# A chain of twelve layers on one core: first fetches and filter preparation inside the first stage, two middle stages joined in one block

## The reference

```
x = _layernorm(x + _L0_attn_ref(x, ...))     # stage 0: 16 heads, table of relative biases
x = _layernorm(x + _L0_xattn_ref(x, ...))    # stage 1: top-32 attention, then s4d
x = _layernorm(x + _L0_ffn_ref(x, ...))      # stage 2: slots
x = _layernorm(x + _L1_attn_ref(x, ...))     # stage 3: linear attention, across the 32 sequences
x = _layernorm(x + _L1_xattn_ref(x, ...))    # stage 4: 8 heads of 64, cross attention
...
def s4d(x, log_dt, A_re, A_im, C_re, C_im, D_skip):
    dtA = dt[:, None] * A
    dC = C * (jnp.exp(dtA) - 1.0) / A
    powers = jnp.exp(dtA[:, :, None] * jnp.arange(L))
    K = 2.0 * jnp.einsum('dn,dnl->dl', dC, powers).real
```

## Time and profile before

| | |
|---|---|
| median of 3 runs | 3241.17 us (3241.14 to 3243.67) |
| the profiled execution | 3240.98 us, its span 3239.2 us |
| PE busy | 2693.2 us (83%) |
| DVE busy | 1952.7 us (60%) |
| ACT busy | 1381.1 us (43%) |
| POOL busy | 1318.9 us (41%) |

### The profile page before, as it was taken

One profiled execution on the slowest core, in us unless ns is written; L12 is line 12 of the kernel. 1 busy time (PEld: TensorE's weight loads), 2 busy tenths in 40 slices (PEclk: granted clock), 3 DMA queues, 4 the chain that ended last, 5 costly groups with the idle time before them and its releaser, 6 DMA issues. The chain is left out here.

```text
span 3239.2 us, 78330 instructions
## 1 busy us (share of the span) xinstructions
PE 2693.2 (83%) x31738; PEld 1918.6 (59%) x31745; DVE 1952.7 (60%) x5135; ACT 1381.1 (43%) x3100; POOL 1318.9 (41%) x1379
## 2 busy tenths in 40 slices
PE   6992566666676999899899986998979999979986
PEld 3551333444534776565799975566357777755665
DVE  5997999355763444566544444564856666635665
ACT  4551556354444554344322213553134444425544
POOL 3451556263311112554233333453843333334546
PEclk9996677687787999899899997998999999989988
DMA  3000000400000000100000000001000000000000
GB/s 105 3 2 1 1 1 1 106 11 1 7 1 34 2 2 2 42 2 3 8 1 1 1 1 17 2 2 44 1 6 2 2 2 2 2 8 2 3 1 27
DMA packets 25350, 37.31 MB, mean 12 GB/s; under 512 B 696, under 2 KB 22336, under 8 KB 24128
## 3 DMA queue, kind: packets, MB, share of 16 engines
q1 hardware_dynamic: 24992, 32.30, 3.2%
HBM read 30.07 MB, written 2.23 MB: 10 GB/s over the span
## 5 line engine op out<-in xcount | busy, mean ns | idle before, releaser
L1205 POOL TENSOR_TENSOR L_attn__qk<-L_attn__turned 128x512 f32<-128x512 f32 x128 | 161.7, 1274 | 300.6 <-DVE L_attn__turned L1316 300.6
L787 DVE TENSOR_REDUCE L_xattn__nm<-psum 128x8 bf16<-128x1024 f32 x128 | 156.4, 1224 | 149.5 <-PE psum L982 143.3
L4346 PE MATMUL psum<-L_ffn__e_hT,weights 128*128 128x256 f32 x1024 | 244.8, 383 | 0.0
L1316 DVE TENSOR_TENSOR L_attn__turned<-psum,weights 128x1024 f32<-128x1024 f32 x128 | 153.4, 1218 | 91.8 <-PE psum L1423 88.8
L4346 PEld LDWEIGHTS psum<-L_ffn__e_hT,weights 128*128 128x128 f32 x1024 | 186.8, 192 | 20.6
L4200 DVE TENSOR_TENSOR L_ffn__e_a<-L_ffn__e_sg,psum 128x512 f32<-128x512 f32 x128 | 88.0, 687 | 176.6 <-ACT L_ffn__e_sg L4192 176.5
L4192 ACT ACTIVATE L_ffn__e_sg<-psum 128x512 f32<-128x512 f32 x128 | 76.5, 598 | 258.7 <-PE psum L4346 258.7
L727 ACT ACTIVATE L_xattn__pT<-psum 128x1024 f32<-128x1024 f32 x128 | 124.0, 1021 | 58.8 <-PE psum L1010 58.8
L4359 PEld LDWEIGHTS psum<-weights,L_ffn__e_a 128*128 128x128 f32 x1024 | 134.4, 191 | 7.3 <-DVE L_ffn__e_a L4200 0.7
L1423 PE MATMUL psum<-L_attn__xT,weights 128*128 128x256 f32 x512 | 136.2, 399 | 2.0 <-DVE L_attn__turned L1316 1.3
L4359 PE MATMUL psum<-weights,L_ffn__e_a 128*128 128x128 f32 x1024 | 135.1, 275 | 0.5 <-DVE L_ffn__e_a L4200 0.5
(11 more groups left out here) (680 smaller groups left out, 7512.9 us busy)
## 6 DMA issues: line engine op xcount, KB each, us to landing
L_xattn__conv_toeplitz<-s4d_kernel SPq DMA_DIRECT2D x5, 1024.0 KB, 10.5
weights<-pack SPq DMA_DIRECT2D x1, 3328.0 KB, 10.6
weights<-pack SPq DMA_DIRECT2D x1, 3140.0 KB, 9.9
weights<-s4d_kernel SPq DMA_DIRECT2D x3, 1024.0 KB, 9.1
weights<-pack SPq DMA_DIRECT2D x1, 2370.0 KB, 9.0
out_dram<-X SPq DMA_DIRECT2D x8, 256.0 KB, 2.3
weights<-pack SPq DMA_DIRECT2D x1, 1732.5 KB, 14.5
ctxT<-ctxT_in SPq DMA_DIRECT2D x1, 1536.0 KB, 18.7
```

What stands on the lines that cost most here:

```text
L787: nc.vector.tensor_reduce(nm[:, n % 2, :].rearrange("p (g c) -> p g c", g=4)[:, 2 * u:2 * u + 2, 0:4], scores[u].rearrange("p g (i q) -> p ...
L1205: nc.gpsimd.tensor_tensor(qk[:, p % 2, u], turned[:, g % 2, :, 0:2 * P], turned[:, g % 2, :, 2 * P:4 * P], ALU.add).then_inc(qk_sb, 1)
L1316: nc.vector.tensor_tensor(turned[:, g % 2], proj[u % 2].unsqueeze(1).to_broadcast([P, 2, 4 * P]), k.w(name + "rope").rearrange("p (t q) -> ...
L4346: last = nc.tensor.matmul(bank[g % 2][:, 256 * c:256 * c + 256], k.w(name + w)[:, o:o + P], hT, start=True, stop=True)
```

## The change

It has three parts, and all twelve stages compute the same as before.

1. `load_stage` is gone. Its work stands in a class `Opening`, whose pieces stage 0's engines run. The packed tensor is cut finer ("const", "s4d", "bias", "later"), SP issues the first pair of X and the small pieces ahead of the bias tables, and the wait for each transfer stands at its first use.
2. The preparation block of stage 1 is gone. DVE works out the angles ahead of stage 0's loop (`dve_angles`), ACT takes sine and cosine once in the loop (`act_waves`), and all else (the powers, the coarse factors, the small tables) goes to POOL, cut into parts 1 to 14: part p stands in POOL's queue of stage 0 behind `with_bias(p + 1)`.
3. Stages 3 and 4 share one block. The statistics, roots and outputs of stage 3's units 1 to 7 (`TurnedTail`) move into stage 4's queues: unit 1 ahead of its loop, units 2 to 7 in it at fixed places. The residuals are written into YT, which holds all units.

The diff, cut to its core:

```diff
+    @contextmanager
+    def one_block(self):
+
+        with ExitStack() as memory, self.nc.Block() as block:
+            self.shared = (memory, block)
+            yield
+        self.shared = None
...
-def load_stage(k):
-
-    nc = k.nc
-    with nc.Block() as block:
-
-        @block.sync
-        def _(sp):
-            k.load_weights(sp, "const")
-            k.load_weights(sp, STAGES[0])
-            xs = k.x.rearrange("b t d -> t b d")
-            sp.dma_start(k.X[:, 0:8, :], xs[:, 0:8, :]).then_inc(k.x_loaded, 16)
-            sp.dma_start(k.X[:, 8:NB, :], xs[:, 8:NB, :]).then_inc(k.x_rest, 16)
-            sp.dma_start(k.ctxT[:], k.ctxT_dram).then_inc(k.ctx_loaded, 16)
...
+    def sync(self, sp):
+        k = self.k
+        xs = k.x.rearrange("b t d -> t b d")
+        k.load_weights(sp, "const")
+        sp.dma_start(k.X[:, 0:2, :], xs[:, 0:2, :]).then_inc(k.x_first, 16)
+        k.load_weights(sp, "s4d")
+        k.load_weights(sp, 0)
+        k.load_weights(sp, "bias")
+        sp.dma_start(k.X[:, 2:8, :], xs[:, 2:8, :]).then_inc(k.x_loaded, 16)
+        sp.dma_start(k.X[:, 8:NB, :], xs[:, 8:NB, :]).then_inc(k.x_rest, 16)
+        sp.dma_start(self.mask_keys[:], k.masks[1][0].rearrange("(u j) g -> u (j g)", j=4)).then_inc(self.masks_in, 16)
+        sp.dma_start(self.mask_text[:], k.masks[0]).then_inc(self.masks_in, 16)
+        k.load_weights(sp, "later")
+        sp.dma_start(k.ctxT[:], k.ctxT_dram).then_inc(k.ctx_loaded, 16)
...
+    def act_waves(self, act):
+        scalar = self.k.nc.scalar
+        act.wait_ge(self.angles, 1)
+        scalar.activation(self.mag[:], self.a_re[:], ACT.Exp)
+        scalar.activation(self.sn[:], self.ang[:], ACT.Sin)
+        scalar.activation(self.cs[:], self.cang[:], ACT.Sin).then_inc(self.waves, 1)
...
+    def pool_part(self, pool, p):
+        k, nc, w, NN, FINE = self.k, self.k.nc, self.w, self.NN, self.FINE
+        tt, ts, copy = nc.gpsimd.tensor_tensor, nc.gpsimd.tensor_scalar, nc.gpsimd.tensor_copy
+        pw, ws = self.pw, self.ws
+
...
+        def multiplied(a, b, m):
+            q = [t[:, 0:m * NN].rearrange("p (m n) -> p m n", n=NN) for t in self.prod]
+            tt(q[0], a[0], b[0], ALU.mult)
+            tt(q[1], a[1], b[1], ALU.mult)
+            tt(q[2], a[0], b[1], ALU.mult)
+            link(tt(q[3], a[1], b[0], ALU.mult))
+
+        def combined(out, m):
+            q = [t[:, 0:m * NN].rearrange("p (m n) -> p m n", n=NN) for t in self.prod]
+            tt(out[0], q[0], q[1], ALU.subtract)
+            link(tt(out[1], q[2], q[3], ALU.add))
...
+        if p == 2:
+            pool.wait_ge(self.waves, 1)
+            pool.wait_ge(self.inverse, 1)
+            tt(pw[0][:, 1, :], self.mag[:], self.cs[:], ALU.mult)
+            link(tt(pw[1][:, 1, :], self.mag[:], self.sn[:], ALU.mult))
+            ts(self.z1[:], pw[0][:, 1, :], 1.0, None, ALU.subtract)
+            link(ts(self.conj[:], w("A_im"), -1.0, None, ALU.mult))
+            times([one(a[:]) for a in self.g], (one(self.z1[:]), pw[1][:, 1:2, :]),
+                  (one(w("A_re")), one(self.conj[:])), 1)
+            for c in range(2):
+                last = tt(self.gi[c][:], self.g[c][:], self.inv[:], ALU.mult)
+            link(last)
+            for c in range(2):
+                last = ts(self.h[c][:], self.gi[c][:], 2.0, None, ALU.mult)
+            link(last)
+            times([a[:, 0:1, :] for a in ws], [one(a[:]) for a in self.h], (one(w("C_re")), one(w("C_im"))), 1)
+        if p == 3:
+            times([a[:, 2:3, :] for a in pw], *doubled(1), 1)
+            times([a[:, 3:5, :] for a in pw], *doubled(2), 2)
+        if p == 4:
+            times([a[:, 5:9, :] for a in pw], *doubled(4), 4)
+        if p == 5:
+            multiplied(*doubled(8), 8)
+        if p == 6:
+            combined([a[:, 9:17, :] for a in pw], 8)
+            times([a[:] for a in self.q2], q, q, 1)
+        if p == 7:
+            times([a[:] for a in self.q4], [a[:] for a in self.q2], [a[:] for a in self.q2], 1)
+            coarser(1, q)
+        if p == 8:
+            coarser(2, [a[:] for a in self.q2])
+        if p == 9:
+            coarser(4, [a[:] for a in self.q4])
...
+                            if opening:
+                                opening.pool_part(pool, p)
...
+                if opening:
+                    pe.wait_ge(k.loaded["const"], 16)
+                else:
+                    pe.wait_ge(k.loaded[stage], 16)
+                    if not rope:
+                        value_bias()
                 turn(0)
+                if opening:
+                    pe.wait_ge(k.loaded[stage], 16)
                 if cross:
                     pe.wait_ge(k.ctx_loaded, 16)
                 if rope:
...
+                if bias:
+                    act.wait_ge(k.loaded["bias"], 16)
+                    nc.scalar.activation(bias16[:], k.w(name + "bias_qk"), ACT.Copy).then_inc(bias16_sb, 1)
...
+                sp.wait_ge(*before.weights_read)
...
+                    pool.wait_ge(before.x_out, p // 2 + 1)
...
+                before.root(pool, 1)
                 for p in range(NB // 2):
+                    if p + 2 in LATE:
+                        before.root(pool, p + 2)
...
+                before.block_out(act, 1)
...
-                        for s in range(2):
-                            evict_v(p + 1, s)
+                        evict_v(p + 1, 0)
+                        for u, at in LATE.items():
+                            if n == at + 3:
+                                before.block_out(act, u)
+                        evict_v(p + 1, 1)
...
+                before.shifted(dve, 1)
                 maxima(0)
                 for n in range(NB):
                     if n + 1 < NB:
                         maxima(n + 1)
+                    for u, at in LATE.items():
+                        if n in (at, at + 1):
+                            before.statistics(dve, range(4 * u + 2 * (n - at), 4 * u + 2 * (n - at) + 2))
+                        if n == at + 2:
+                            before.shifted(dve, u)
                     inverted(n)
...
+                    pe.wait_ge(before.x_out, p // 2 + 1)
+                    if p == 0:
+                        pe.wait_ge(before.res_sb, 3)
...
+    def statistics(self, dve, sequences):
+        vector = self.k.nc.vector
+        for i in sequences:
+            dve.wait_ge(self.res_sb, i // 4 + 1)
+            vector.bn_stats(self.st[:, i, :], self.r[:, i, :]).then_inc(self.halves, 1)
+        for i in sequences:
+            dve.wait_ge(self.halves, i + 1)
+            vector.bn_aggr(self.mv[:, i, :], self.st[:, i, :]).then_inc(self.moments, 1)
+
+    def root(self, pool, u):
+        k, gpsimd = self.k, self.k.nc.gpsimd
+        pool.wait_ge(self.moments, 4 * u + 4)
+        gpsimd.tensor_tensor(self.rstd[:, u, 0, :], self.mv[:, 4 * u:4 * u + 4, 1],
+                             k.eps[:, 0:1].to_broadcast([P, 4]), ALU.add).then_inc(self.var_eps, 1)
+        pool.wait_ge(self.var_eps, u + 1)
+        gpsimd.tensor_tensor(self.rstd[:, u, 1, :], self.rstd[:, u, 0, :], k.neg_half[:, 0:1].to_broadcast([P, 4]),
+                             ALU.pow).then_inc(self.rstd_sb, 1)
+
+    def shifted(self, dve, u):
+        dve.wait_ge(self.rstd_sb, u + 1)
+        dve.wait_ge(self.moments, 4 * u + 4)
+        self.k.nc.vector.scalar_tensor_tensor(out=self.shift[:, u, :], in0=self.mv[:, 4 * u:4 * u + 4, 0], scalar=-1.0,
+                                              in1=self.rstd[:, u, 1, :], op0=ALU.mult,
+                                              op1=ALU.mult).then_inc(self.shift_sb, 1)
+
+    def block_out(self, act, u):
+        act.wait_ge(self.shift_sb, u + 1)
+        for j in range(4):
+            last = self.k.nc.scalar.activation(self.k.X[:, 4 * u + j, :], self.r[:, 4 * u + j, :], ACT.Identity,
+                                               bias=self.shift[:, u, j:j + 1], scale=self.rstd[:, u, 1, j:j + 1])
+        last.then_inc(self.x_out, 1)
...
-                sp.wait_ge(y_ps, BLOCKS)
+                sp.wait_ge(y_ps, BLOCKS // 2)
...
-                    nc.vector.tensor_tensor(r[:, u % 2], k.bank[u][:].rearrange("p (j d) -> p j d", j=4),
-                                            k.X[:, 4 * u:4 * u + 4, :], ALU.add).then_inc(res_sb, 1)
...
+                    units = slice(4 * u, 4 * u + 4)
+                    nc.vector.tensor_tensor(YT[:, units, :], k.bank[u][:].rearrange("p (j d) -> p j d", j=4),
+                                            k.X[:, units, :], ALU.add).then_inc(res_sb, 1)
+
+                residual(0)
+                tail.statistics(dve, range(0, 4))
+                residual(1)
+                residual(2)
+                tail.shifted(dve, 0)
+                residual(3)
+                residual(4)
+                tail.statistics(dve, range(4, 8))
+                residual(5)
+                residual(6)
+                residual(7)
...
-
-                        m = 1
```

(24 more changed lines are left out.)

486 lines of the change are left out of this document (249 added, 237 removed).

## The result

The changed kernel takes 3186.09 us (median of 4 runs, 3182.48 to 3196.24) against 3241.15 us for the kernel before on the same chip: a ratio of 0.9828, 95% interval 0.9815 to 0.9841, that is 52 to 60 us less. Forecast were 3183 us.

A forecast was written before the change was run, and what follows sets the result against it. It took stage 0's loop to be bound by DVE, with idle stretches at the start, before stage 1 and before stage 4. Terms -11.7 + 1.0 - 31.9 + 10.8 - 24.8 - 1.6 + 0.3 = -57.9 gave 3183 us, range 3176 to 3191.

The forecast's parts named there:

- start: Stage 0's opening: first bias matmul at about 12.2 us instead of 23.93, -11.7 (bounds -12.5 to -9).
- sine and cosine on ACT: Stage 0's loop: the table load back to the exponential delays the next eviction of maxima, +1.0 (0 to 2.6).
- preparation block: Between stages 0 and 1: stage 1 starts at 261.0 instead of 292.88, -31.9.
- POOL's parts: Stage 0's loop: parts longer than 3.7 us delay k16m, PE and DVE, +10.8 (bounds +3 to +20).
- join: Stages 3 to 4: PE starts stage 4 at 989.3 instead of 1014.08, -24.8.
- warmer PE, late norms: Stage 4: first projections at the high clock, -1.6; norms fit loop gaps, +0.3 with longer semaphore clearing.
- the rival that DVE and POOL hold each other up: Stage 0's loop while a part runs: up to 30 of 53 us come on top, 3213 us; chance 0.04.
- the slack: Stage 0's loop: 1.2 + 2.5 = 3.7 us of POOL work fit ahead of k16m before anything moves.
- the start that gains little: Stage 0's opening: small transfers with 512-byte rows hold up the bias, 3192 to 3195 us; chance 0.06.
- the cheaper parts: Stage 0's loop: POOL's parts cheaper and hidden, their term 3, 3175 us; chance 0.15.
- the dear dependent instruction: POOL in stage 0: fixed cost per dependent instruction, 0.4 us more each adds 36 us (3219); chance 0.03.
- the join that gives less: Stage 4: late norms stretch its loop or first pairs wait for X, 3192 us; chance 0.12.

The follow-up runs named there:

- the experiment with two blocks: The changed kernel with stages 3 and 4 in blocks of their own again, all eight units normalised ahead of stage 4: 3214.46 us, ratio 0.9903.
- the filling: The changed kernel with 14 short unread matmuls put into PE's 2.2 us wait in each block of stage 3's loop: 3182.65 us, ratio 0.9819.

## Why the prediction was right in the sum, and where it was not

Terms against the profiled execution, in us:

```
                         forecast   measured
start                     -11.7      -8.3   (23.93 -> 15.66)
sine and cosine on ACT     +1.0       0.0
preparation block         -31.9     -31.7   (-24.6 at stage 1's start, less 7.2)
POOL's parts              +10.8     +15.5   (7.2 + 8.3)
join                      -24.8     -25.0   (26.20 -> 1.18)
warmer PE, late norms      -1.3      -1.7   (289.4 -> 287.8 from stage 4 to 5)
clock in stages 1 to 3      -        +6.1   (-24.6 -> -18.5 at stage 3's end)
start of stages 7 and 10    -        -4.9   (8.93 -> 6.50, 7.49 -> 5.05)
clock in the last stages    -        +5.3   (+0.4 with the row above)
sum                       -57.9     -44.7
```

**Right in part by luck.** The six terms of the forecast, as measured here, come to -51.2 us in the place of -57.9: that would be 3190, still within the range. Two steps were sized wrongly, the start by 3.4 us and POOL's parts by 4.7. Against that stands a gain that no term has. Stages 7 and 10 run the code of stage 0, and in it DVE's wait until POOL has cleared the tile vz now stands behind DVE's first copy and no longer ahead of it. PE at the start of stage 7, before and after:

```profile
2016.23 0.98 PE L1068 MATMUL psum<-weights 128*128 128x1 f32 x4 [8.93 <-DVE L_xattn__bvw L862]
```
```profile
1971.46 0.98 PE L1310 MATMUL psum<-weights 128*128 128x1 f32 x4 [6.50 <-DVE L_xattn__bvw L1102]
```

PE starts each of the two stages 2.4 us sooner, -4.9 in all. Stage 7 doesn't keep it: it is 230.0 us long in place of 227.5, with 37 us at the low clock in place of 28. That the forecast of 3183 is within 3 us of the median owes something to errors that run against each other.

**The block and the join** were right to 0.2 us. Both were idle time of PE with one cause, read from two rows each, and the experiment with two blocks confirms the join by undoing it (25.0).

**The start** failed in two steps. "The bias is in at 10.0": it came at 12.73, and 2.7 of the 3 us that I had kept for finer pieces as a bound were needed. From 3 to 6 us, when the small pieces were under way, the DMA engines moved 240 GB/s, where it was 446 before, and from 2 to 12 us 307 in place of 373; some 0.5 MB of other sequences had moved by then as well. What of this the short rows cost, and what the number of transfers, is not tested. And "projection, keys and the angle chain on DVE lie in the wait for the bias tables": the chain does not, since POOL's products held it to 15.06, and in this profile that takes the term past its bound of -9. I had the rival that DVE and POOL hold each other up, but looked for it in the loop, where DVE's long steps read PSUM, and not here. The Trainium skill's "SBUF — State Buffer", section "Who interferes with whom", has the rule: the two share one pair of ports, and a VectorE instruction in a fast mode or with two inputs from SBUF waits out a GpSimd instruction that got there first. The rows agree, with 1.93, 1.82, 1.77 and 1.84 beside a product and 0.18 to 0.22 without. The loop agrees too, with its sums at 1.21 us beside a part: one input is from PSUM.

**ACT's sine and cosine** cost nothing. The masked keys of the pair behind them start at 42.99 where before they started at 51.15, the same 8.2 us ahead as at the start. The second table load falls into the wait for the biased scores.

**POOL's parts** are the term that was mis-sized. The lengths were right, 6.6, 4.45, 4.2, 4.9, 4.4, 3.7, 2.65, 4.3, 3.35, 3.0, 5.35 and 3.9 us against 6.9 to 2.8 forecast, all a little high, and so was the slack: parts 7, 8, 10 and 11 moved nothing. Over 3.7 us they come to 8.4. What the sum lacked is what PE does behind a wait: part 2 cost 5.0 us in the place of 3.2, as PE waited 3.43 and then ran its matmuls at half the clock, in a loop where PE is nearly as busy as DVE. The parts 5, 9 and 12 show the same, 2.6, 1.8 and 2.9 us where 1.2, 0.6 and 1.65 stand over the slack, and in this profile these four pairs are the ones of the parts in which the clock fell. Part 9 sets the two costs apart: PE waits 1.1 us behind it in all six profiles with the parts in this place, and its pair was 0.7 us longer in five of them and 1.8 in this one, the only one in which the clock fell behind its wait. I had written that a delay isn't carried on, and priced the wait alone.

**The late norms** fit into their gaps, as argued. Of the rivals, the start that gains little has 3.4 of its 9 to 12 us; the cheaper parts, the dear dependent instruction and the join that gives less are refuted by the rows above, and of the one in which DVE and POOL hold each other up there is some 1 us, in another place.

**The clock outside the places changed** was in no term. Stage 3 has taken 109 to 117.4 us in twelve profiles, stage 0's first pair 13.1 to 17.1, stage 6 79.1 to 82.3, stage 9 534.9 to 538.6, all by how much of them fell to the low clock. In the profile of before, most of them are short; in the first of the changed kernel, most long. That a change which shifts everything by 45 us draws them anew, and that they make the 3181 to 3196 us of one program, I take from this; no run tests it. The Trainium skill's "TensorE: Matmul & The Clock Gate", section "HAM oscillation — how this bites in real kernels", describes such a clock that falls in PE's waits; that it falls in waits of 2.2 us these traces show, and the filling shows them to be the cause of most of it in stage 3. What decides for one execution which waits count I can't tell from them. That stays open.

## What to carry to other kernels

Work moved to an engine that is off the path goes ahead of that engine's longest wait, not into its shortest: the same 53 us of instructions cost 15 us behind the bias addition and nothing ahead of the norm. A late operand for PE costs its delay, and if the clock falls behind the wait, 1.2 to 2.2 us more (parts 2, 5, 9 and 12); give such a term a range for it. A wait that is moved in code shared by several stages changes all of them: look for the other stages before the sum is made. And a gain of 2 to 3 us ahead of a long chain of stages may be there in the rows and gone from the total, so measure such an edit by the rows, and over several executions.

## What the runs showed of the hardware that I had not expected

- A VectorE instruction of 0.2 us on 64 elements took up to 1.93 when a GpSimd product was running, and was done within 0.1 us of it (two instructions in each of eight profiles). Stage 3's loop has it too, before and after the change: eight of the 32 instructions that write L_attn__phi take 0.92 us and not 0.28, each of them beside a GpSimd product of 1.26 us, and they stand ahead of PE's waits of 2.2 us.
- In stage 3's loop PE's clock fell to half in or behind single waits of 2.22 us, all seven in one profile and three of seven in another; behind one of them the matmul of 0.44 us took 0.67 two rows later.
- The issue of the key mask's transfer (4.62 to 15.60 us) held SyncE's queue for 10.98 us, and with it everything issued behind it; here nobody was waiting for that. Whether it is the transfer or its place is open: the context's issue took 7.76 us in the kernel before, behind the transfers of the start, and 0.43 us now, behind this one.
- GpSimd products of 64 elements took 0.30 us and followed each other every 0.27; with a wait for the engine's own result between them it was 0.38. The fixed cost that I feared is 0.1 us.
